# A windowed-attention layer on one core: two moves within a tile's slot, and another order of the prologue with two query buffers

## What is computed

```python
q = (x @ Wq.T + bq).reshape(B, S, N_HEADS, D_K)        # k, v likewise, x layernormed
scores = jnp.einsum('bqhd,bkhd->bhqk', q, k) * SCALE
mask = (j <= i) & (j >= i - 128)
scores = jnp.where(mask, scores, jnp.float32(-10000.0))
attn = jax.nn.softmax(scores, axis=-1) + jnp.float32(1e-09)
ctx = jnp.einsum('bhqk,bkhd->bqhd', attn, v).reshape(B, S, D_MODEL)
...
x = x + ctx @ Wo.T + bo
x = x + jnp.einsum('bsi,oi->bso', layernorm(x), jnp.sign(weight))
```

## Time and profile before

| | |
|---|---|
| time, median of 3 runs | 806.22 us (798.45 to 813.16) |
| the profiled execution's own time | 802.16 us |
| its span, first to last instruction | 800.4 us |
| mean granted TensorE clock | 0.965 of full |
| busy share of PE, DVE, ACT, POOL | 88%, 62%, 62%, 57% |
| DMA queue of the kernel | 93440 packets, 80.42 MB, 59.5% of 16 engines |
| PE waits for exponentials (line 962 for line 543) | 38.4 us in 33 waits |

### The profile page before, as it was taken

The page is one execution under the profiler, slowest core; times in us unless marked ns, Lnnn a source line. Parts: engine busy times, 40 slices in busy tenths (PEclk is TensorE's granted clock), DMA queues, the critical chain, the costliest instruction groups (busy, mean ns, idle before and its releaser), DMA issues.

```text
span 800.4 us, 31430 instructions
## 1 busy us (share of the span) xinstructions
PE 707.4 (88%) x13076; PEld 596.4 (75%) x13076; DVE 494.1 (62%) x1044; ACT 493.4 (62%) x1061; POOL 459.0 (57%) x649
## 2 busy tenths in 40 slices
PE   4478999899999999999988999998999999999985
PEld 3366877777788777778777777877777887778773
DVE  4555665666666666666566656666656666666634
ACT  3257675666666666676657666566666666566651
POOL 7835664576646556556555655555664645655763
PEclk9789999999999999999999999999999999999999
DMA  4977565675566557566766755774655766754431
GB/s 117 112 100 122 87 113 106 106 125 105 108 108 115 112 98 120 99 107 114 117 110 104 122 106 90 115 119 94 119 101 97 122 105 103 121 104 91 79 51 41
DMA packets 94940, 83.73 MB, mean 105 GB/s; under 512 B 10416, under 2 KB 94800, under 8 KB 94800
## 3 DMA queue, kind: packets, MB, share of 16 engines
q1 hardware_dynamic: 93440, 80.42, 59.5%
q10 hardware_dynamic: 1360, 1.31, 0.5%
HBM read 18.22 MB, written 8.39 MB: 33 GB/s over the span
## 4 chain that ended last, share of the span: by engine, by line
PE 68%; ACT 9%; DVE 9%; issue 6%; DMA 1%; SPq 1%; ACTq 0%; DVEq 0%
PE gc L830 16%; PE sc L962 14%; PE pv L980 14%; PE ga L830 6%; PE ga L991 5%; PE mx L919 4%; DVE nmax L682 4%; PE mx L925 3%; DVE k_lo L670 3%; ACT xn L480 3%; ACT u L601 2%; ACT prob L543 2%; PE gc L845 2%; ACT k_hi L510 2%; PE gb L1020 2%
## 5 line engine op out<-in xcount | busy, mean ns | idle before, releaser
L543 ACT ACTIVATE prob<-sc 128x512 f32<-128x512 f32 x448 | 264.0, 596 | 186.3 <-PE sc L962 184.4
L962 PE MATMUL sc<-q_stack,k_stack 128*128 128x256 f32 (+1 forms) x1024 | 227.9, 314 | 40.6 <-ACT prob L543 38.4
L682 DVE TENSOR_REDUCE nmax<-mx 128x6 f32<-128x960 f32 x188 | 195.4, 1040 | 95.4 <-PE mx L925 93.9
L962 PEld LDWEIGHTS sc<-q_stack,k_stack 128*128 128x128 f32 x1024 | 158.9, 195 | 76.6 <-ACT prob L543 47.5
L429 POOL TENSOR_SCALAR ve<-mv 128x1 f32<-128x1 f32 x64 | 14.1, 221 | 245.2 <-DVE mv L774 245.2
L980 PE MATMUL pv<-prob,v_ones 128*32 128x128 f32 x3840 | 147.0, 280 | 0.5 <-issue 0.4
L416 POOL TENSOR_SCALAR_AFFINE_SELECT prob<-prob 128x1024 f32<-128x1024 f32 x128 | 139.7, 1092 | 13.0 <-ACT prob L545 13.0
L413 POOL TENSOR_SCALAR_AFFINE_SELECT prob<-prob 128x1024 f32<-128x1024 f32 x112 | 122.4, 1093 | 41.9 <-ACT prob L543 41.7
L980 PEld LDWEIGHTS pv<-prob,v_ones 128*32 128x32 f32 x3840 | 94.2, 110 | 26.2 <-issue 1.5
L925 PE MATMUL mx<-k_max,q_stack 16*32 16x160 bf16 x4008 | 70.7, 231 | 0.8 <-issue 0.8
L662 DVE SCALAR_TENSOR_TENSOR q_lo<-gc,bq,q_hi 128x256 fp32r<-128x256 f32 x64 | 28.0, 479 | 50.1 <-ACT q_hi L499 50.1
(11 more groups left out here) (141 smaller groups left out, 1425.5 us busy)
## 6 DMA issues: line engine op xcount, KB each, us to landing
q_stack<-q_hi SPq DMA_DIRECT2D x128, 128.0 KB, 4.2
k_stack<-k_hi SPq DMA_DIRECT2D x128, 128.0 KB, 4.6
xs<-x SPq DMA_DIRECT2D x32, 256.0 KB, 4.5
q_stack<-q_lo SPq DMA_DIRECT2D x64, 128.0 KB, 4.6
k_stack<-k_lo SPq DMA_DIRECT2D x64, 128.0 KB, 4.8
xr<-x SPq DMA_DIRECT2D x64, 128.0 KB, 2.0
out<-x SPq DMA_DIRECT2D x64, 128.0 KB, 2.0
k_max<-k SPq DMA_DIRECT2D x64, 64.0 KB, 2.6
```

Source lines behind the costliest of these rows:

```text
L543: a.activation(prob[:, own:nxt + 1:nxt - own, 2 * f:2 * f + 2, :], sc, ACT.Exp, scale=SCALE).then_inc(exp_done, 1)
L682: v.tensor_reduce(nmax[:, n % 2, :].rearrange("p (r h) -> p r h", r=C)[:, :, h0:h0 + m], banks[:, :, 0:WIN * m].rearrange("p r (h k) -> p ...
L962: last = mm(sc_bank[f % 2][:, 2 * P * j:2 * P * j + q], k_stack[:, h, ak:ak + P], q_stack[:, h % HB, P * t:P * t + q], start=True, stop=True)
```

## The change

In the slot, TensorE does `max_scores(.., 0)` and `prob_v(.., 0)` ahead of fill 1, and `turn_max` behind it; ACT does `nmax_part` behind exponential 1 in place of ahead of it, and `norm1` ahead of exponential 6. `q_hi` and `q_lo` have two buffers each, and `q_part` waits for the stacking of the pair two before. `stack_q` is now in three parts r (high, high, low; two DMAs each), of which the first has a semaphore of its own, `q_headed`; `max_scores` waits for that one alone, `scores` for the other two parts. In the prologue, SP issues all of pair 0 ahead of pair 1 and loads pair 2's rows first; POOL clears `k_stack` ahead of the rest of `q_stack`, and fills `v_ones` in DVE's place; DVE computes the signs early and takes the maxima of tile 0 ahead of the low parts of pair 1, those of tile 1 and 2 right behind them; the projection of pair 1's keys goes to `pv_bank`; the maxima of tile 2 use `mx_banks` alone; and some of TensorE's waits move from the prologue's end to where their data are used.

```diff
--- before.py
+++ after.py
@@ -89,8 +89,8 @@
         xt_lo = sb("xt_lo", [P, C, 2 * P], F32R)
-        q_hi = sb("q_hi", [P, C, 2 * P], F32R)
-        q_lo = sb("q_lo", [P, C, 2 * P], F32R)
+        q_hi = sb("q_hi", [P, 2, C, 2 * P], F32R)
+        q_lo = sb("q_lo", [P, 2, C, 2 * P], F32R)
         k_hi = sb("k_hi", [P, 2, C, 2 * P], F32R)
@@ -142,6 +142,7 @@
         x_loaded = [sem("x_loaded0"), sem("x_loaded1")]
+        q_headed = [sem("q_headed0"), sem("q_headed1")]
         q_stacked = [sem("q_stacked0"), sem("q_stacked1")]
@@ -240,20 +241,21 @@
-            def stack_q(b, p, c):
+            def stack_q(b, p, r):
                 i, _ = halves(p)
...
                 g = PAIRS * b + p
+                src = (q_hi, q_hi, q_lo)[r]
+                stacked = q_stacked[i] if r else q_headed[i]
...
                     sp.wait_ge(q_zeroed, 1 if g == 0 else 2)
-                sp.wait_ge(q_hi_done, g + 1)
-                sp.wait_ge(q_lo_done, g + 1)
-                for r, src in enumerate((q_hi, q_hi, q_lo)):
+                sp.wait_ge(q_lo_done if r == 2 else q_hi_done, g + 1)
+                for c in range(C):
                     at = 64 * c + DK * r
                     sp.dma_start(q_stack[at:at + DK, :, cols].bitcast(F32),
-                                 src[:, c, :].bitcast(F32)).then_inc(q_stacked[i], 16)
+                                 src[:, g % 2, c, :].bitcast(F32)).then_inc(stacked, 16)
...
             def set_k_max(b, p):
@@ -299,8 +301,8 @@
                 if part["k"]:
-                    for c in range(C):
-                        stack_q(*part["k"], c)
+                    for r in range(3):
+                        stack_q(*part["k"], r)
                 if part["ks"]:
@@ -327,18 +329,20 @@
                 sp.dma_start(dst[:, :], src).then_inc(b_loaded, 16)
-            for c in range(C):
-                stack_q(0, 0, c)
+            load_x(0, 2)
+            stack_q(0, 0, 0)
+            stack_q(0, 0, 1)
             set_k_max(0, 0)
-            load_x(0, 2)
-            for c in range(C):
-                stack_q(0, 1, c)
-            set_k_max(0, 1)
+            stack_q(0, 0, 2)
             sp.wait_ge(ones_done, 1)
...
             stack_k(0, 0)
+            stack_q(0, 1, 0)
+            set_k_max(0, 1)
             stack_nmax(0, 0)
+            stack_q(0, 1, 1)
             stack_nmax(0, 1)
+            stack_q(0, 1, 2)
             load_x(0, 3)
@@ -451,9 +455,10 @@
             make_windows(1)
+            g.memset(k_stack[:, :, 0:2 * P].bitcast(F32), 0.0).then_inc(k_zeroed, 1)
             g.memset(q_stack[:, :, 2 * P:].bitcast(F32), 0.0).then_inc(q_zeroed, 1)
-            g.memset(k_stack[:, :, 0:2 * P].bitcast(F32), 0.0).then_inc(k_zeroed, 1)
             rsqrt1(0, 2)
+            g.memset(v_ones[:, :, :, DK:], 1.0).then_inc(memset_done, 1)
             sum_v(0, 0)
@@ -493,10 +498,11 @@
-                if g > 0:
-                    act.wait_ge(q_stacked[(g - 1) % 2], 96 * ((g - 1) // 2 + 1))
-                for c in range(C):
-                    last = a.activation(q_hi[:, c, :], bank[:, 2 * P * c:2 * P * (c + 1)], ACT.Identity, bias=bq[:, c:c + 1])
+                if g > 1:
+                    act.wait_ge(q_headed[g % 2], 32 * (g // 2))
+                    act.wait_ge(q_stacked[g % 2], 64 * (g // 2))
+                for c in range(C):
+                    last = a.activation(q_hi[:, g % 2, c, :], bank[:, 2 * P * c:2 * P * (c + 1)], ACT.Identity, bias=bq[:, c:c + 1])
                 last.then_inc(q_hi_done, 1)
...
             def k_part(b, p, bank=gc):
@@ -556,10 +562,10 @@
                     exp(b, t, 0)
+                    exp(b, t, 1)
                 if part["nm"]:
...
                 if now:
-                    exp(b, t, 1)
                     exp(b, t, 2)
@@ -588,10 +594,10 @@
                     q_part(*part["tqv"])
-                if now:
-                    exp(b, t, 6)
                 if part["ln"]:
                     norm1(*part["ln"])
+                if now:
+                    exp(b, t, 6)
                 if part["pv"]:
@@ -618,7 +624,7 @@
             q_part(0, 1)
-            k_part(0, 1, gb)
+            k_part(0, 1, pv_bank)
             k_16_part(0, 1)
@@ -659,8 +665,8 @@
                 for c in range(C):
-                    last = v.scalar_tensor_tensor(q_lo[:, c, :], bank[:, 2 * P * c:2 * P * (c + 1)], bq[:, c:c + 1],
-                                                  q_hi[:, c, :].bitcast(F32), ALU.add, ALU.subtract)
+                    last = v.scalar_tensor_tensor(q_lo[:, g % 2, c, :], bank[:, 2 * P * c:2 * P * (c + 1)], bq[:, c:c + 1],
+                                                  q_hi[:, g % 2, c, :].bitcast(F32), ALU.add, ALU.subtract)
                 last.then_inc(q_lo_done, 1)
...
             def k_part(b, p, bank=gc):
@@ -788,34 +794,37 @@
+            def mx_turn(t, i):
+                return (mx_banks, sc_banks)[(MXG * t + i) % 2 if t < 2 else 0]
+
             stats1(0, 0)
...
             xt_part(0, 0, sc_bank[0])
+            split_w(1, "k")
             stats1(0, 1)
-            split_w(1, "k")
-            v.memset(v_ones[:, :, :, DK:], 1.0).then_inc(memset_done, 1)
             split_w(2, "v")
+            dve.wait_ge(w_loaded["f"], 16)
+            v.tensor_scalar(w_pos, w_raw["f"], 0.0, None, ALU.is_gt)
+            v.tensor_scalar(w_neg, w_raw["f"], 0.0, None, ALU.is_lt).then_inc(w_sign_done, 1)
             q_part(0, 0)
+            dve.wait_ge(w_sign_done, 1)
+            v.tensor_tensor(w_sign[:, :, :], w_pos, w_neg, ALU.subtract).then_inc(w_sign_done, 1)
             k_part(0, 0, gb)
...
             stats1(0, 2)
+            for i in range(MXG):
+                row_max(0, 0, i, mx_turn(0, i))
             q_part(0, 1)
+            k_part(0, 1, pv_bank)
+            for i in range(MXG):
+                row_max(0, 1, i, mx_turn(1, i))
+            xt_part(0, 2, pv_bank)
+            for i in range(MXG):
+                row_max(0, 2, i, mx_turn(2, i))
+            q_part(0, 2)
             dve.wait_ge(b_loaded, 64)
             v.scalar_tensor_tensor(bvs[:, :], bv[:, :], ROWS * SPREAD, bv[:, :], ALU.mult, ALU.add).then_inc(bvs_done, 1)
-
-            dve.wait_ge(w_loaded["f"], 16)
-            v.tensor_scalar(w_pos, w_raw["f"], 0.0, None, ALU.is_gt)
-            v.tensor_scalar(w_neg, w_raw["f"], 0.0, None, ALU.is_lt).then_inc(w_sign_done, 1)
-            k_part(0, 1, gb)
-            dve.wait_ge(w_sign_done, 1)
-            v.tensor_tensor(w_sign[:, :, :], w_pos, w_neg, ALU.subtract).then_inc(w_sign_done, 1)
-            for t in range(3):
-                for i in range(MXG):
-                    row_max(0, t, i, (mx_banks, sc_banks)[(MXG * t + i) % 2])
-                if t == 1:
-                    xt_part(0, 2, pv_bank)
-            q_part(0, 2)
             dve.wait_ge(bvs_done, 1)
@@ -888,6 +897,8 @@
                     pe.wait_ge(v_done, n + 1)
+                    if n == 2:
+                        pe.wait_ge(q_lo_done, 3)
                 elif m == 0:
@@ -901,7 +912,7 @@
                 if i == 0 and t % 2 == 0:
-                    pe.wait_ge(q_stacked[t // 2 % 2], 96 * (PAIRS // 2 * b + t // 4 + 1))
+                    pe.wait_ge(q_headed[t // 2 % 2], 32 * (PAIRS // 2 * b + t // 4 + 1))
                     pe.wait_ge(k_max_set[g % 2], 32 * (g // 2 + 1))
@@ -946,7 +957,7 @@
                             i, m = halves(tt // 2)
-                            pe.wait_ge(q_stacked[i], 96 * (PAIRS // 2 * b + m + 1))
+                            pe.wait_ge(q_stacked[i], 64 * (PAIRS // 2 * b + m + 1))
                     if t % 2 == 0:
@@ -967,6 +978,8 @@
                 if i == 0:
+                    if n == 0:
+                        pe.wait_ge(memset_done, 2)
                     pe.wait_ge(prob_masked, 2 * n + 1)
@@ -1037,6 +1050,7 @@
             def sum_signs():
...
                 pe.wait_ge(v_done, 3)
+                pe.wait_ge(w_sign_done, 2)
                 for c in range(C):
@@ -1053,6 +1067,8 @@
             def bias_proj(b):
...
                 pe.wait_ge(cb_step, 3 * (b + 1))
+                if b == 0:
+                    pe.wait_ge(w_lo_done, 4)
@@ -1070,14 +1086,14 @@
                     scores(b, t, 0)
-                if part["nm"]:
-                    turn_max(*part["nm"])
-                if now:
-                    scores(b, t, 1)
                 if mx:
...
                     prob_v(*pv, 0)
+                if now:
+                    scores(b, t, 1)
+                if part["nm"]:
+                    turn_max(*part["nm"])
                 if op:
@@ -1147,28 +1163,26 @@
             both(q_proj, 0, 1)
-            both(k_proj, 0, 1, gb)
-            pe.wait_ge(memset_done, 2)
+            both(k_proj, 0, 1, pv_bank)
+            pe.wait_ge(memset_done, 1)
             pe.wait_ge(windows_done, 6)
...
                 for i in range(MXG):
-                    max_scores(0, t, i, (mx_banks, sc_banks))
```

(9 more changed lines are left out.)

## The result

The changed kernel takes 750.37 us (median of four runs, 745.87 to 754.61), the kernel before 806.97 in the same comparison: a ratio of 0.933, 95% interval 0.922 to 0.944. Its profiled execution took 747.88 us, span 746.1, mean granted clock 0.984; against before's 802.16 and 800.4 at 0.965 that is 54.3 us of span to account for.

The account below looks back on a forecast made before the run. TensorE, busy 88% of the span, was taken as the bound, its idle time as what reordering can win. 802.2 less 36.5 (boundary), 17 (clock) and 4 (prologue), plus 1.5 (small waits), gave 746 us; range 736 to 766.

Parts of the forecast that it names:

- The boundary stall: Steps from even into odd slots: fill 1's 1.27 or 1.40 us wait for exponential 7 goes whole, 28 times, 36.5 us.
- What is late next: Same boundary: `k_max` has 1.0 us of margin, at worst 0.1; the masked probabilities are 1.8 us ahead; 1.5 us added.
- The 1.5 us of small waits: Added over all boundaries for `k_max` landing late; bounds 0 and 6 us.
- The second stall: Middle of even slots, behind the key projection: the maxima's 13.9 us of waits for DVE stay, as nothing ahead changes.
- The clock: Main part: hardly one of eleven half-clock stretches stays once the stalls ahead go, 17 us; rival that they stay, 763 us, 0.12.
- The prologue: Before slot 0: earlier loads and reordered work start slot 0 4 us earlier; bounds 7 earlier and 2 later.
- Its first term: Prologue: DVE's first row maximum follows the first fill, 5.6 us earlier; bounds 4 and 6.6.
- The serial banks: Prologue: tile 2's maxima, with one set of banks, take 5.4 us in place of 3.05, 2.3 us lost.
- The slower rival: Boundary: the wait for `k_max`, landing up to 6.1 us after issue, replaces the stall; 826 us, chance 0.03.

Follow-up runs that it names:

- max_first: The changed kernel with DVE's row maximum of group 1 ahead of the keys' low part `k_lo`: 746.53 us, 0.926 of the kernel before.
- norm_only: The kernel before with one move alone, ACT's `norm1` ahead of exponential 6: 763.5 us, 0.949 of the kernel before.
- pe_only: The kernel before with TensorE's maxima and values ahead of fill 1, `turn_max` behind, `nmax_part` behind exponential 1; `norm1` not moved: 768.18 us, 0.955.
- kmax_late: The changed kernel with ACT's copy `k_16_part`, and so `k_max`, behind exponential 5: 777.6 us, 0.965 of the kernel before.
- prologue_only: The changed kernel with the old slot order on TensorE and ACT; new prologue, two query buffers and parted stacking alone: 804.21 us, 0.999 of before.
- kmax_later: The changed kernel with ACT's copy `k_16_part`, and so `k_max`, behind `norm1`, ahead of exponential 6: 824.45 us, 1.024 of the kernel before.
- values_banks: max_first with values ahead of first maxima, pair 1's high queries and `k_max` issued earlier in the prologue, tile 2's maxima in both bank sets: 737.61 us, 0.913.

## Why the prediction was right

The forecast was 746 us from the profiled execution's 802.2, and the same execution of the changed kernel took 747.9; the median is 750.4, inside the range. By its steps:

- **The boundary stall, 36.5 us.** Right: 37.9 us of waits for exponentials are gone. All that was worked out from the rows is in the timeline after: ACT's idle time filled but for 0.81 (0.7 were expected), `nmr` there in time, no wait at fill 1.
- **What is late next.** Right for `k_max` (3.6 us needed from the issue, 3.7 given; landings of 2.7 at the median and 3.6 at most, so nothing is lost). Incomplete otherwise: the copy `u`, which frees the values' bank, was not on the list. It costs nothing with both moves, and 15.7 us with PE's alone. The 1.5 us of small waits were 3.4, and at other places: `cx`, `k_stack` and `t_lo`, not `k_max`.
- **The second stall stays.** Right, 13.9 us before and after; max_first shows that all but 0.6 us of it come from the order on DVE alone, and that only some 4 us are to be had before `k_max` is late.
- **The clock, 17 us.** Right in size: 10 stretches net, 17.0 us. That the stalls are the cause was an argument from the eleven places; the runs bear it out from both sides. Between 100 and 700 us stretches are absent where the stalls at the boundary are 0 (after), 0.34 (norm_only), 0.56 (pe_only) or 0.9 us at the mean (kmax_late), and there where they are 1.16 (before, eleven up to 730 us), 1.2 (prologue_only, 37.6/31, fourteen) or 1.7 us (kmax_later, twelve), whichever engine or DMA makes them. The profiled executions do not stand alone in this: over all runs that the ratios use, the clock of the whole span is 0.944 to 0.965 in the kernel before, 0.946 to 0.959 in prologue_only and 0.934 to 0.950 in kmax_later, and 0.967 to 0.989 in every other kernel here. That PE is busier does not bring them: it is 97% busy from 100 to 700 us at a clock of 1.00. The rule of the Trainium skill that was weighed against (page "TensorE: Matmul & The Clock Gate", section "HAM oscillation — how this bites in real kernels"), which ties a fall to gaps as long as a whole wait for a DMA, would have left the clock as it was; norm_only goes against it for this kernel, and so does prologue_only, whose longest stall in the list is 1.4 us. What decides between the stalls that are followed by a stretch and those that are not stays open (31 stalls, 14 stretches in prologue_only). The length of a single stall does not decide it alone: five of 1.30 to 1.76 us in kmax_late have none behind them.
- **The prologue, 4 us.** Its first term was undersized (6.6 us at the row maximum, 5.6 taken) and its price more so: slot 0 came 2.3 us earlier. The serial banks cost less than was said, 1.5 us and not 2.3 (from 37.12 to 41.70 us, 4.6 against 3.05; values_banks, without them, begins slot 0 1.4 earlier). What was missing is the 6.2 us that pair 1's `k_max` takes behind the stacking ahead of it, a wait of 3.73 us. The prediction had looked at that DMA for the slots only. Alone, this part can't be told from no change in the time; it shows in where slot 0 begins.
- **The slower rival** (826 us by `k_max` in the stall's place) did not come, for the reason given; kmax_later makes it happen, at 824.

The sum is as near as it is in part because its errors cancel. Against the forecast's terms the boundary gave 1.4 us more and the clock 1.8 more (18.8 us less busy in the ledger's first window), the prologue 1.7 less and the small waits 1.9 less; the end of the kernel, which had no term, took 1.2. Together that is 1.6 us less than the 56 forecast, and the span shows 54.3.

## What to carry to other kernels

When an in-order engine makes another wait, look whether it was idle just ahead of the string that is late, and move what needs nothing of that string into the idle time; then list every buffer that the moved work frees or needs (here `u` and `k_max`), each with its margin from the rows. A short stall that repeats can cost more than its length, if the granted clock falls behind it: look at the windows behind such stalls, and make one the length of the old stall by other means to see it come back. And a DMA's time to land has to be read where it will be issued: 64 KB took 2.7 us in the slots and 6.2 behind a queue in the prologue.

## What was not expected of the hardware

- The clock's dependence on the stall's length at one place is steep: 29 stalls of 0.9 us at the mean (kmax_late) gave one fallen stretch, behind the longest of them, and 31 of 1.2 us (prologue_only) gave fourteen.
- POOL's reciprocal root in the prologue took 3.09 us before, with DVE's fill of `v_ones` (1.76 us from 13.37) and then a subtraction of two operands (0.63 from 15.05) beside it, and 0.79 after, when that fill was moved; in the slots it takes 0.71 for the same shape. It is 3.09 in all four profiles with the prologue of before and 0.79 in those with the new one. The subtraction starts 1.9 us behind the root, when 0.79 us would long be over, so the fill is the likelier cause; it was not tried by itself. The rows of before and, in the second fence, of after:

```profile
13.16 3.09 POOL L386 TENSOR_TENSOR rs<-ve,half 128x2 f32<-128x2 f32 x1
```
```profile
14.05 0.79 POOL L390 TENSOR_TENSOR rs<-ve,half 128x2 f32<-128x2 f32 x1
```
